# Key products of a half's second token tile placed between the Gram products of the half before

## The reference: linear attention over 16 images

```
xn = group_norm(x)                        # 32 groups of 8 channels
q, k, v = split(xn^T @ qkv_w^T + qkv_b)   # tokens x 256 each
k = relu(k + pos_enc);  q = relu(q)       # 8 heads of 32 channels
z   = 1 / (q . sum_tokens(k) + 1e-6)
kv  = k^T v   (per head)
out = (q kv) * z
y = x + (out @ proj_w^T + proj_b)
```

## Time and profile before

| | us |
|---|---|
| median of 3 runs | 2628.76 (2627.99 to 2630.11) |
| time of the profiled execution | 2629.6 |
| its span in the trace | 2627.5 |
| TensorE matmul busy | 2568.3, 98% |
| VectorE, ScalarE, GpSimd busy | 1515.9, 1698.8, 1979.7 |

### The profile page before, as it was taken

How to read it: one execution, slowest core, us unless ns; L and a number is a source line. 1 busy time by engine, 2 the same in 40 slices (tenths; PEclk the granted TensorE clock), 3 DMA queues, 4 the chain that set the end, 5 groups by cost and what they waited for, 6 DMA issues and landing times.

```text
span 2627.5 us, 45059 instructions
## 1 busy us (share of the span) xinstructions
PE 2568.3 (98%) x15940; PEld 2203.1 (84%) x15940; DVE 1515.9 (58%) x2405; ACT 1698.8 (65%) x2705; POOL 1979.7 (75%) x1234
## 2 busy tenths in 40 slices
PE   4999999999999999999999999999999999999998
PEld 3878888888888888888888888888888888888886
DVE  5656555565555556555555555656555555554547
ACT  4766766666666666766667666666666666666654
POOL 4958778687787778868687786887768778687875
PEclk9999999999999999999999999999999999999999
DMA  7547867677776867767777677786867677676658
GB/s 257 191 159 254 271 223 264 233 259 254 239 268 225 274 227 260 260 238 256 234 268 261 225 262 251 248 272 222 264 236 263 234 255 258 234 247 205 229 197 300
DMA packets 324189, 642.15 MB, mean 244 GB/s; under 512 B 25728, under 2 KB 47104, under 8 KB 323968
## 3 DMA queue, kind: packets, MB, share of 16 engines
q1 hardware_dynamic: 323968, 639.28, 72.6%
HBM read 519.25 MB, written 119.93 MB: 243 GB/s over the span
## 4 chain that ended last, share of the span: by engine, by line
PE 91%; issue 2%; DVE 2%; POOL 2%; DMA 2%; ACT 1%; SPq 0%; DVEq 0%; ACTq 0%; POOLq 0%
PE banks L603 21%; PE banks L627 20%; PE banks L663 19%; PE banks L615 13%; PE banks L617 7%; PE banks L594 6%; PE banks L648 3%; DMA q<-in_x 1%; PE banks L678 1%; DVE zt L937 1%; POOL hl L1301 0%; POOL kacc L1315 0%; DMA y<-xr 0%; PE banks L685 0%; POOL posb L1326 0%
## 5 line engine op out<-in xcount | busy, mean ns | idle before, releaser
L1315 POOL TENSOR_TENSOR kacc<-kacc,kt 128x512 f32<-128x512 f32 x368 | 477.7, 1298 | 277.3 <-ACT kt L1119 275.5
L1301 POOL TENSOR_TENSOR hl<-xn,hl 128x512 fp32r<-128x512 f32 x384 | 488.9, 1296 | 217.6 <-ACT hl L1102 217.5
L603 PE MATMUL banks<-wqk,hl 128*128 128x256 f32 x4608 | 645.0, 289 | 7.3 <-POOL hl L1301 7.3
L869 DVE TENSOR_TENSOR xt<-banks,xt 128x512 fp32r<-128x512 f32 x400 | 274.9, 687 | 590.0 <-ACT xt L1107 589.7
L627 PE MATMUL banks<-hl,wqk 128*128 128x512 f32 x2304 | 600.0, 396 | 0.2 <-ACT zt L1154 0.2
L615 PE MATMUL banks<-kk,xt 128*128 128x512 f32 x1600 | 583.8, 399 | 3.3 <-DVE kk L885 3.3
L603 PEld LDWEIGHTS banks<-wqk,hl 128*128 128x128 f32 x4608 | 575.0, 191 | 9.1 <-POOL hl L1301 9.1
L663 PE MATMUL banks<-uhl,mhl 128*128 128x512 f32 (+1 forms) x2316 | 541.8, 383 | 2.1 <-DVE xr L899 2.1
L663 PEld LDWEIGHTS banks<-uhl,mhl 128*128 128x128 f32 x2316 | 423.6, 188 | 89.9 <-issue 2.5
L1338 POOL TENSOR_TENSOR q<-q,zb 128x1024 f32<-128x1024 f32 x180 | 433.8, 2410 | 74.5 <-DMA zb<-z_rows 74.4
L627 PEld LDWEIGHTS banks<-hl,wqk 128*128 128x128 f32 x2304 | 406.7, 188 | 92.0 <-issue 1.3
(11 more groups left out here) (120 smaller groups left out, 2341.5 us busy)
## 6 DMA issues: line engine op xcount, KB each, us to landing
posb<-pos_plus_bk SPq DMA_DIRECT2D x375, 256.0 KB, 5.0
xs<-in_x SPq DMA_DIRECT2D x184, 512.0 KB, 6.9
xa<-in_x SPq DMA_DIRECT2D x184, 512.0 KB, 6.0
xr<-in_x SPq DMA_DIRECT2D x184, 512.0 KB, 3.9
zb<-z_rows SPq DMA_DIRECT2D x184, 512.0 KB, 6.0
y<-xr SPq DMA_DIRECT2D x184, 512.0 KB, 7.0
z_rows<-zt SPq DMA_DIRECT2D x32, 256.0 KB, 5.5
xr<-in_pos SPq DMA_DIRECT2D x25, 256.0 KB, 4.7
```

The lines of the kernel that those rows point to most:

```text
L603: last = mm(psK[:, par(n, h), i * C:(i + 1) * C], hl_of(t)[:, a, c, s:s + P], wqk[:, w, c, C:2 * C], start=(j == 0), stop=(j == len(terms) ...
L869: v.tensor_tensor(xt[:, hp, 1, :, :].rearrange("p i n -> p (i n)"), psT, xt[:, hp, 0, :, :].rearrange("p i n -> p (i n)"), ALU.subtract).t ...
L1301: g.tensor_tensor(hl_of(t)[:, 1, :, s], xn_of(n, t)[:, :, s], hl_of(t)[:, 0, :, s], ALU.subtract).then_inc(xl_ready, 1)
L1315: g.tensor_tensor(both, both, kt[:, par(n, h), :], ALU.add).then_inc(ks_done, 1)
```

## The change

The function `transpose_and_k` is split: `transpose` keeps the transposes and the two waits behind them, and `keys_and_gram` issues the keys of half h together with the Gram products of the half before. Seven key products go first (all six of tile 0 and the first of tile 1), then come the Gram products' waits, and then the eight Gram products with the other five key products between them. `k_done` is signalled by the last key product, which now stands in front of the last two Gram products. The very first half has no Gram product beside it and keeps its keys alone. In step t = 0 of an image the key sums (`key_sums`) now come behind the Gram products and not ahead of them. The numbers, shapes and operands of the matmuls are as before, and the lists of the other engines are the same.

```diff
-            def transpose_and_k(n, h):
+            def transpose(n, h):
...
                 pe.wait_ge(xl_ready, half_no(n, h))
                 wait(pe, kr_ready, half_no(n, h) - 2)
-                for i in range(TILES):
-                    s = tok + i * P
-                    terms = [(c, a, w) for c in range(CC) for a, w in ((0, 0), (0, 1), (1, 0))]
-                    for j, (c, a, w) in enumerate(terms):
-                        last = mm(psK[:, par(n, h), i * C:(i + 1) * C], hl_of(t)[:, a, c, s:s + P], wqk[:, w, c, C:2 * C],
-                                  start=(j == 0), stop=(j == len(terms) - 1))
-                last.then_inc(k_done, 1)
...
+            def key_product(n, h, i, j):
+
+                s = h % 2 * HALF + i * P
+                c, a, w = ((0, 0, 0), (0, 0, 1), (0, 1, 0), (1, 0, 0), (1, 0, 1), (1, 1, 0))[j]
+                return mm(psK[:, par(n, h), i * C:(i + 1) * C], hl_of(h // 2)[:, a, c, s:s + P], wqk[:, w, c, C:2 * C],
+                          start=(j == 0), stop=(j == 5))
...
+            def gram_waits(n, h):
                 if h == 0:
                     wait(pe, gt_ready, n)
                 pe.wait_ge(xtl_ready, half_no(n, h))
                 pe.wait_ge(kl_ready, half_no(n, h))
...
+            def keys_and_gram(n, h, gn, gh):
+
+                for j in range(6):
+                    key_product(n, h, 0, j)
+                key_product(n, h, 1, 0)
+                gram_waits(gn, gh)
+                for i in range(TILES):
+
+                    if i == 1:
+                        key_product(n, h, 1, 3)
+                    gram_high(gn, gh, i, 0)
+                    key_product(n, h, 1, 3 * i + 1)
+                    gram_low(gn, gh, i, 0)
+                    keys_last = key_product(n, h, 1, 3 * i + 2)
+                    if i == 1:
+                        keys_last.then_inc(k_done, 1)
+                    gram_high(gn, gh, i, 1)
+                    gram_last = gram_low(gn, gh, i, 1)
+                gram_last.then_inc(g_done, 1)
...
             def step(n, t):
-                transpose_and_k(n, 2 * t)
+                transpose(n, 2 * t)
                 if t:
-                    gram(n, 2 * t - 1)
+                    keys_and_gram(n, 2 * t, n, 2 * t - 1)
                 elif not first(n):
-                    gram(n - 1, NHB - 1)
+                    keys_and_gram(n, 2 * t, n - 1, NHB - 1)
+                else:
+                    keys(n, 2 * t)
...
                 if t < LAST:
-                    transpose_and_k(n, 2 * t + 1)
+                    transpose(n, 2 * t + 1)
+                    keys_and_gram(n, 2 * t + 1, n, 2 * t)
                     if t == 0 and not first(n):
                         wait(pe, out_ready, two_no(n - 2, LAST - 2, CC - 1))
                         key_sums(n - 1, psX[:, 1])
-                    gram(n, 2 * t)
```

More of the change, by code:

```diff
@@ L598, in transpose_and_k, with gram_high, gram_low @@
                 wait(pe, kr_ready, half_no(n, h) - 2)
-                for i in range(TILES):
-                    s = tok + i * P
-                    terms = [(c, a, w) for c in range(CC) for a, w in ((0, 0), (0, 1), (1, 0))]
-                    for j, (c, a, w) in enumerate(terms):
-                        last = mm(psK[:, par(n, h), i * C:(i + 1) * C], hl_of(t)[:, a, c, s:s + P], wqk[:, w, c, C:2 * C],
-                                  start=(j == 0), stop=(j == len(terms) - 1))
-                last.then_inc(k_done, 1)
-            def gram(n, h):
+            def key_product(n, h, i, j):
[3 more added lines that the diff above has]
+                          start=(j == 0), stop=(j == 5))
+            def gram_high(n, h, i, c):
+                hp = par(n, h)
+                mm(psG[:, c, :], xt[:, hp, 0, i, c * P:(c + 1) * P], kk[:, hp, i, :, :],
+                   start=(h == 0 and i == 0), stop=False)
+            def gram_low(n, h, i, c):
+                hp = par(n, h)
+                return mm(psG[:, c, C:2 * C], xt[:, hp, 1, i, c * P:(c + 1) * P], kk[:, hp, i, 0, :],
+                          start=False, stop=(h == NHB - 1 and i == TILES - 1))
+            def gram_waits(n, h):
                 if h == 0:
@@ L611, in gram, with keys @@
                 pe.wait_ge(kl_ready, half_no(n, h))
-                hp = par(n, h)
+            def gram(n, h):
+                gram_waits(n, h)
                 for i in range(TILES):
                     for c in range(CC):
[L615 to L618, removed]
+                        gram_high(n, h, i, c)
+                        last = gram_low(n, h, i, c)
                 last.then_inc(g_done, 1)
+            def keys(n, h):
+                for i in range(TILES):
+                    for j in range(6):
+                        last = key_product(n, h, i, j)
+                last.then_inc(k_done, 1)
+            def keys_and_gram(n, h, gn, gh):
+                for j in range(6):
+                    key_product(n, h, 0, j)
+                key_product(n, h, 1, 0)
+                gram_waits(gn, gh)
+                for i in range(TILES):
+                    if i == 1:
[9 more added lines that the diff above has]
+                gram_last.then_inc(g_done, 1)
             def query(n, t, m, bank):
```

## The result

| | us | to the kernel before |
|---|---|---|
| before | 2629.36 (4 runs) | |
| changed | 2655.77 (2655.18 to 2656.52, 4 runs) | 1.0105, 95% interval 1.0091 to 1.0118 |
| predicted | 2656 (2641 to 2676) | |

The ratio comes with its 95% interval; the quotient of the two medians is 1.0100, inside it. What follows is the page of the changed kernel, then TensorE's waits (who waited for whom, us in total, times, longest). The last row is the same wait in the kernel before.

The account below looks back on a forecast made before the run. TensorE, holding a matmul in 98% of the span, was taken to bound the kernel. Terms 19.7 + 1.1 + 3 + 4.2 + 0 = 28 us on the median 2628.8 gave 2656.8, stated as 2656, range 2641 to 2676.

Parts of the forecast that it names:

- The join: Step t = 1 of images 2 to 15: late `k_done` runs through VectorE's reciprocals; TensorE waits 1.41 us each, 19.7 us.
- the late signal: In each half, `k_done` comes 1.06 us later, with three 512s and three 256s ahead of the last key product.
- the early wait: Gram products want to start 0.60 us earlier, as five key products no longer stand ahead of them.
- Image 1: At its join the chain is the bound already, so the whole delay goes through: 1.1 us.
- Ordinary odd halves: Halves such as 13: `key_add` slips by 0.82 us, Gram products still have 0.6 to spare, no loss.
- Halves 15 and 23: Behind two statistics blocks or the next image's reciprocal root: about 0.1 us each, 15 images, 3 us.
- Image 0: Short steps without output products: 2.7 us in two first halves, 1.0 in half 20, 0.5 in half 16; together 4.2.
- the loop: Image 0: a low-key wait also holds back five key products and `k_done`; somewhat over 1.06 us in two halves, 2.7.
- Widths: Mixing 256- and 512-column matmuls in each half: taken as 0, bounds 42 us gained to 25 us lost.
- the chain did not give way anywhere: Rival 2: delay absorbed at the join too, widths give a few us: 2625 to 2634; 6%.
- only-the-join: Rival 3: only the join, image 0 and image 1 wait: 2652, or 2642 if the mixture gains 10 us; 20%.

Follow-up runs that it names:

- selective version: Changed kernel with the old order in image 0, the first 8 halves of image 1, and beside keys of halves 2, 4, 14, 20 of other images: 2619.87 us.
- in twos: Kernel before with the Gram products ordered two of 512 columns, two of 256, two of 512, two of 256: 2613.97 us, 0.9945.
- the version with the key behind one pair: Kernel before with only the last key product, which signals `k_done`, moved behind one Gram pair (a 512 and a 256): 2625.9 us, 0.9988.
- the one with the key behind three pairs: Kernel before with only the last key product, which signals `k_done`, moved behind three Gram pairs: 2650.87 us, 1.0084.

## Why the prediction was right, and where only its sum was

- *The join.* Forecast 1.41 us in 14 images. In the trace the Gram product of half 3 starts 842.25 - 835.06 = 7.19 us behind the keys of half 3, where it was 825.87 - 819.50 = 6.37 (the keys before started at 819.50), 0.82 later; it was to start 0.60 earlier, so TensorE lost 1.42. Putting the keys of half 2 back returned the 1.0 that the late signal was to cost, and left the 0.40 of the early wait. This step is shown. Image 1 lost 2.0 where I had 1.1: besides the delay, which goes through, the earlier wait costs 0.6 there as well and half 1 loses 0.3.
- *Ordinary odd halves.* No wait, as forecast.
- *Halves 15 and 23.* Half 15 lost 0.2 where I had 0.1: the transposes of half 17 in image 5 come 921.96 - 914.35 = 7.61 us behind those of half 16, where an ordinary half takes 7.40. Half 23 lost nothing. In its place I had missed the group norm's product in step 10 (L586): the transposes of half 22 in image 5 come 951.30 - 946.24 = 5.06 us behind those of half 21, where it was 934.20 - 929.39 = 4.81, since ScalarE comes to it late behind the statistics half. Together nearly 0.5 for an image, not 0.2.
- *Image 0.* This term was mis-sized: 4.2 forecast, 9.3 in the trace, 7.3 in the runs. I counted the loop once or twice; TensorE waited for the low keys of halves 0 to 4, of 16 and of 20, and the group norm was behind it. And I put the clock at nothing, which fell to 1.2 GHz twice behind long waits and cost some 3 us.
- *Widths.* The step that failed in kind: "By neighbours the sum doesn't change, and I take 0." For the twenty mixed matmuls this holds (2.93 and 2.92 us). But the queries and outputs behind them became 10 to 20 ns shorter in each series, and over the kernel this is a gain of some 9 us. It is well inside the bounds that I had given (42 gained to 25 lost).
- *GpSimd.* I had no term for the keys' wait for the low part of `xn`. In half 6 of images 7, 13 and 14 it is gone, and with the overlap this is some 4 us. It is gone in the selective version too, where the join isn't late, so the late join is not shown to be its cause; there is one trace of each kernel, and the sum of these waits goes from 2.9 to 7.6 us among them.

The sum was right by luck. By the traces the waits and the clock cost about 38 us and not 28: 20 at the joins, 2 in image 1, 7 in halves 15 and 21, 9.3 in image 0. Against the 10 us more stand the 8.5 of the shorter queries and outputs and the 4 of GpSimd, which leaves 26; the spans differ by 27.0. The join, 20 of the forecast's 28 us, came as worked out and was not luck.

The rivals: the chain did not give way anywhere, only-the-join was too little, and the even cost in each half, which I had not named ahead but tested, is out. The Trainium skill's figures of 262 and 518 cycles (TensorE: Matmul & The Clock Gate, Back-to-back issue gap), 0.109 and 0.216 us, which that section gives for an isolated matmul of 256 and of 512 columns, were reached in no order tried, taken over a series. The best one of 512, the outputs of the version with the 256s first, stands at 2.73 / 12 = 0.2275, and ten keys of 256 at 0.118.

## What to carry to other kernels

When matmuls are mixed to keep TensorE dense, ask first which of them carries the signal that other engines wait for: three pairs of matmuls ahead of one `k_done` cost 21 us with nothing else moved. The price is not set in the ordinary step but at the few places where another engine's list has a long operation behind the waiting one, and these can be found beforehand by following the chain and reading its slack. Where waits grow to 2 us and more, look at the granted clock behind them as well: here it was a third of image 0's loss. And a reordering that leaves its own stretch as long as it was can still shorten the next one, so time whole steps, not the stretch that was edited.

## What the hardware showed that I had not expected

The distance between the starts of 512-column products depends on what stood ahead of them, several products back. The same eight Gram products, 1.41 us long in both orders, give six queries of 1.40 us when they alternate and of 1.37 when the 256s come first, so that 22 products of 512 stand in a row; and the output series that follows the queries is shorter too, 2.73 against 2.75. The time of the whole kernel follows: 2629 us alternating, 2619 with the 512s first, 2614 in twos, 2612 with the 256s first. It is not the number of width changes (nine, three, five, one in a half). A lone 256 between two 512s, four in a half before and none in the three fast orders, goes with the long distances, but it isn't the whole rule either: the version with the key behind one pair and the one with the key behind three pairs both have three of them, and the ordinary step is 12.03 us in the first and 12.11, as before, in the second. What in TensorE does this stays open: no run separated the loading of weights from the supply of instructions or from the order of the operands.
